# A graph layer on one core: denominator weights 32 columns wide, one block of 32 partitions per tile of nodes

## What is computed

```
Q = elu(q) + 1 ;  K = elu(k) + 1
KV = einsum("nshd,nshv->nhdv", K, v)
Z = 1 / (einsum("nlhd,nhd->nlh", Q, K.sum(axis=1)) + 1e-6)
msg = einsum("nlhd,nhdv,nlh->nlhv", Q, KV, Z)
```

## Time and profile before

| | us |
|---|---|
| median of 3 runs | 1503.72 (1503.57 to 1506.25) |
| the profiled execution, its own time | 1505.46 |
| its span, first to last instruction | 1503.7 |
| PE busy | 1414.6 (94%) |
| PEld busy | 1279.9 (85%) |
| DVE busy | 1151.3 (77%) |
| POOL busy | 953.5 (63%) |
| ACT busy | 759.2 (50%) |
| mean granted TensorE clock | 0.986 |

### The profile page before, as it was taken

One profiled execution on the slowest core, in us unless ns is written; L12 is line 12 of the kernel. 1 busy time (PEld: TensorE's weight loads), 2 busy tenths in 40 slices (PEclk: granted clock), 3 DMA queues, 4 the chain that ended last, 5 costly groups with the idle time before them and its releaser, 6 DMA issues.

```text
span 1503.7 us, 26952 instructions
## 1 busy us (share of the span) xinstructions
PE 1414.6 (94%) x9032; PEld 1279.9 (85%) x9032; DVE 1151.3 (77%) x2565; ACT 759.2 (50%) x1339; POOL 953.5 (63%) x873
## 2 busy tenths in 40 slices
PE   5999999679999999999999999999999999999986
PEld 5999999568888888888888888888888888888875
DVE  6777778558878878787788877788777887878873
ACT  4555555235554445644556445554455445554453
POOL 5777775566775666656676567755677556675452
PEclk9999999899999999999999999999999999999998
DMA  5787765121220212202122112211122111220000
GB/s 175 254 266 230 226 217 194 53 60 49 70 70 23 64 52 69 65 24 62 56 69 62 28 48 69 69 41 48 48 69 69 31 55 52 69 67 24 14 14 14
DMA packets 71630, 121.81 MB, mean 81 GB/s; under 512 B 38053, under 2 KB 42786, under 8 KB 71598
## 3 DMA queue, kind: packets, MB, share of 16 engines
q1 hardware_dynamic: 55598, 108.00, 22.7%
q0 software_dynamic: 16000, 13.43, 4.1%
HBM read 69.47 MB, written 51.70 MB: 81 GB/s over the span
## 4 chain that ended last, share of the span: by engine, by line
PE 62%; DVE 21%; ACT 6%; issue 5%; DVEq 4%; POOL 1%; POOLq 1%; DMA 0%; SPq 0%; ACTq 0%
PE psum L222 18%; PE psum L224 18%; PE psum L223 18%; DVE top_e L1108 6%; PE psum L419 4%; DVE qf L1007 2%; DVE qf L1203 2%; ACT qf L775 2%; DVEq L1056 2%; DVE psum L1128 1%; PE psum L662 1%; ACT relu L789 1%; ACT relu L873 1%; ACT s_hi L790 1%; DVE bn_y L902 1%
## 5 line engine op out<-in xcount | busy, mean ns | idle before, releaser
L1349 POOL TENSOR_TENSOR s_lo<-relu,s_hi 128x1000 fp32r<-128x1000 f32 (+1 forms) x50 | 89.9, 1797 | 150.5 <-ACT s_hi L790 150.5
L222 PE MATMUL psum<-w_hi,h_hi 128*125 128x256 f32 x600 | 172.5, 287 | 5.1 <-DVE h_lo L1229 3.7
L224 PE MATMUL psum<-w_hi,h_lo 128*125 128x256 f32 x600 | 170.1, 283 | 0.0
L223 PE MATMUL psum<-w_lo,h_hi 128*125 128x256 f32 x600 | 169.6, 283 | 0.0
L1343 POOL DMA_INDIRECT xg<-table_xt,idx x100 | 124.7, 1247 | 55.1 <-issue 55.1
L863 ACT ACTIVATE z_hi<-qf 128x500 fp32r<-128x500 f32 x50 | 30.2, 622 | 232.2 <-DVE qf L1203 224.3
L1349 POOL TENSOR_TENSOR h_lo<-relu,h_hi 128x1000 fp32r<-128x1000 f32 x50 | 127.4, 2567 | 29.8 <-ACT h_hi L790 29.8
L1146 DVE SCALAR_TENSOR_TENSOR base<-xb,rn,b_bc 125x256 f32<-125x256 f32 x100 | 144.6, 1486 | 0.3
L1345 POOL DMA_INDIRECT ag<-table_al,idx x100 | 121.3, 1213 | 30.5 <-issue 30.5
L222 PE MATMUL psum<-z_hi,w_hi 128*128 128x500 f32 x300 | 119.8, 399 | 2.3 <-DVE z_lo L1177 2.3
L222 PE MATMUL psum<-xT_hi,w_hi 128*128 128x500 f32 x300 | 120.5, 402 | 1.3 <-ACT h_hi L790 1.3
(11 more groups left out here) (231 smaller groups left out, 4754.1 us busy)
## 6 DMA issues: line engine op xcount, KB each, us to landing
xb<-in_x SPq DMA_DIRECT2D x50, 448.0 KB
xT_hi_table<-x1T_hi SPq DMA_DIRECT2D x25, 500.0 KB
xT_lo_table<-x1T_lo SPq DMA_DIRECT2D x25, 500.0 KB
xT_hi<-xT_hi_table SPq DMA_DIRECT2D x25, 500.0 KB
xT_lo<-xT_lo_table SPq DMA_DIRECT2D x25, 500.0 KB
table_xt<-xts SPq DMA_DIRECT2D x25, 455.0 KB
out<-xmid SPq DMA_DIRECT2D x25, 448.0 KB
xb<-in_x SPq DMA_DIRECT2D x50, 52.0 KB
```

Source lines behind the costliest of these rows:

```text
L222: pe.matmul(out, wh, xh, start=first, stop=False)
L223: pe.matmul(out, wh, xl, start=False, stop=False)
L224: return pe.matmul(out, wl, xh, start=False, stop=last)
L1349: ptt(out, src, hi, ALU.subtract).then_inc(S[done], 1)
```

## The change

Each of the four tiles gets 32 partitions of PSUM of its own. `kden` shrinks to 32 columns per chunk, the 8 head columns written four times, and is the same weight for all tiles. The matmul of tile j writes partitions 32j to 32j+31; the two chunks of a tile add up there, and the loops are swapped (chunks outside, tiles inside). Of each 32 partitions the first 8 serve the rounded value, the next 8 the rest, and the others are not selected by `den_sel`. Which partitions hold a rest is told by a new column `low_rows`, -1 there and 0 elsewhere, so that one instruction over all 128 partitions replaces the subtraction over 64: rdenT = rden_hi * low_rows + rden. The column is made once, ahead of phase 2, by two sums and a multiplication.

```
-KD_STEP = P + 16
+QUAD = 32
...
-        kden = sb("kden", [P, CK, T * KD_STEP])
+        kden = sb("kden", [P, CK, QUAD])
+        low_rows = sb("low_rows", [P, T + 1])
...
+        rden_hi = sb("rden_hi", [P, R + 1], F32R)
...
-                for j in range(T):
-                    for q in range(CK):
-                        last = pe.matmul(psum[:, 6, 0:R], kden[:, q, j * P:(j + 1) * P], tile(qf, q, j),
-                                         start=j == 0 and q == 0, stop=j == T - 1 and q == CK - 1)
+                for q in range(CK):
+                    for j in range(T):
+                        last = pe.matmul(psum[j * QUAD:(j + 1) * QUAD, 6, 0:R], kden[:, q, :], tile(qf, q, j),
+                                         start=q == 0, stop=q == CK - 1)
...
             for q in range(CK):
-                for d in (0, 64):
-                    at = kden[:, q, :].rearrange("p (j n) -> p j n", j=T)[:, :, d + q * per:d + (q + 1) * per]
-                    ts(at, head_mask[:, 0:P:MIX_CH].unsqueeze(1).broadcast_to([P, T, per]), kx[:, q, C:C + 1], None,
-                       ALU.mult)
+                at = kden[:, q, :].rearrange("p (d n) -> p d n", n=MIX_HEADS)[:, :, q * per:(q + 1) * per]
+                ts(at, head_mask[:, 0:P:MIX_CH].unsqueeze(1).broadcast_to([P, QUAD // MIX_HEADS, per]),
+                   kx[:, q, C:C + 1], None, ALU.mult)
...
-                    rows = [d + 16 * j + q * per for d in (0, 64)]
+                    rows = [QUAD * j + d + q * per for d in (0, MIX_HEADS)]
...
+            dve.reduce_sum(low_rows[:, 0:T], ident[:].rearrange("p (j r) -> p j r", r=QUAD)[:, :, MIX_HEADS:2 * MIX_HEADS],
+                           AXX)
+            dve.drain()
+            dve.reduce_sum(low_rows[:, T:T + 1], low_rows[:, 0:T], AXX)
+            dve.drain()
+            ts(low_rows[:, T:T + 1], low_rows[:, T:T + 1], -1.0, None, ALU.mult)
...
-                dve.tensor_copy(rdenT[:, 0:R], rden)
-                dve.drain()
-                tt(rdenT[64:P, 0:R], psum[64:P, 6, P:P + R], rdenT[64:P, 0:R], ALU.subtract).then_inc(S["den_rows"], 1)
+                dve.tensor_copy(rden_hi[:, 0:R], rden)
+                dve.drain()
+                stt(rdenT[:, 0:R], rden_hi[:, 0:R], low_rows[:, T:T + 1], rden, ALU.mult,
+                    ALU.add).then_inc(S["den_rows"], 1)
```

## The result

| | before | changed kernel |
|---|---|---|
| median of 4 runs, us | 1503.67 (1503.57 to 1506.25) | 1511.84 (1510.76 to 1513.25) |
| ratio of the times | | 1.0051, interval 1.0033 to 1.0068 |
| the profiled execution, us | 1505.46 | 1510.76 |
| its span, us | 1503.7 | 1509.0 |
| mean granted clock in it | 0.986 | 0.978 |

The changed kernel is slower by 0.5%, where 1% faster was forecast; the time lies outside the range. Line 1126 of the changed kernel is another instruction, a COPY in `top_weights` that was 1119.

A forecast was written before the change was run, and what follows sets the result against it. Bound by a chain through POOL's e_lo, DVE's line 1108 and ACT that ends PE's 1.5 us hole. -15.4 us (22 x 0.70) + 0.3 us = -15.1 us, from 1503.72 to 1488.6 us; range 1481 to 1504.6.

The forecast's parts named there:

- What bounds the kernel: Each step is set by POOL's e_lo, DVE's line 1108 in top_weights (4.08 us, mostly standing), ACT, then PE.
- the hole: PE's recurring 1.5 us wait before the gb matmuls of line 662, for ACT's gate rows; forecast to shrink to 1.1 us.
- The matmuls: Denominator's 16 records on PE: overlapping tiles gain 0.81 us, a drain takes 0.2, so the denominator is done 0.6 us earlier.
- If 1108 is ahead of `e_lo` it takes 0.17 us: DVE in top_weights: line 1108 passes before POOL's subtractions, line 1114 stands instead till 692.97; 0.75 us gained.
- the -15.4 us: Whole gain in the steps: 22 standing instances of line 1108 times 0.70 us.
- the 0.70 us per step: Gain taken at DVE's line 1108, between branches of 0.75 and 0.62 us, passing on whole to PE's restart.
- The other branch of the forecast: Line 1108 comes up to some 0.35 us into the first e_lo and is let in between the two; 0.62 us gained.
- The new three-operand instruction: On DVE after the denominator, replaces a subtraction of 0.29 us; +0.03 us, not held up beside e_lo.
- Once: Three small DVE instructions ahead of g_lo cost 0.6 us, stage b's first full step gains about 0.3; together +0.3 us.
- Rival 3: At PE's hole: if it outgrows 1.5 us, the clock falls, 22 x 1.6 = 35 us, 1539 us; chance 0.05.
- Rival 1: Denominator matmuls do not overlap, 1108 still ends with e_lo, PE's loss goes into the hole; 1504.3 us; chance 0.26.

The follow-up runs named there:

- e8: Changed kernel with GpSimd's two e_lo subtractions waiting for gate_rows, until the weights of the experts are out; 1439.45 us, ratio 0.9566.
- e9: Kernel before the change with GpSimd's two e_lo subtractions waiting for gate_rows; 1464.25 us, ratio 0.973.
- e5: Changed kernel with the two matmul loops back in the old order, tiles outside and chunks inside; 1511.37 us, one run.
- e6: Changed kernel with all 8 narrow matmuls sent to partitions 0 to 31, leaving out the denominators of three tiles; 1504.0 us, one run.
- e3: Changed kernel with the 8 narrow matmuls issued three times; 1501.99 us, ratio 0.9978.
- e4: Kernel before the change with only the new three-operand instruction and its column low_rows, weights still 128 wide; 1501.17 us, ratio 0.9973.
- e7: Changed kernel with only line 1115, the first instruction of top_weights, moved ahead of one_over_den; 1483.62 us, ratio 0.9862.
- e2: Changed kernel with all of top_weights called ahead of one_over_den on DVE; 1588.12 us, ratio 1.0554.
- e1: Kernel before the change with all of top_weights called ahead of one_over_den on DVE; 1559.89 us, ratio 1.0377.

## Why the prediction was wrong

- **What bounds the kernel: right.** The chain over line 1108 and the hole were read rightly; e8 and e9 show that the hole goes when that line is free. But the prediction called what fills PE ahead of the hole unimportant "as long as the hole is there". It is not unimportant to the clock.
- **The matmuls: mis-sized.** The forecast let two tiles overlap and took 8 x 0.107 us from first to last record. Four overlap: each tile has four records of its own, 0.11 to 0.13 us apart, and the last of 16 starts 0.36 us after the first. The denominator's next reader, line 1133, starts at 0.97 us, not 1.4. The order of the loops, on which the step leaned, gives 0.02 us (e5). The cost of the changes of mode was taken as 0.2 and 0.3 us; it is 0.09 (the matmul before now starts 0.32 us ahead, not 0.23) and 0.17 us (0.20 from the last record to the next matmul, not 0.03; e6 has the same 0.20). So PE saves 1.05 us per step, not 0.3. The Trainium skill ("TensorEngine Tiling (Array Packing)", Key Properties) says that tiles run independently and that a change of mode drains the engine; the trace agrees with both, at those prices.
- **The step that failed: "If 1108 is ahead of `e_lo` it takes 0.17 us", and the -15.4 us built on it.** It came ahead in every step, by 0.15 to 0.29 us, and took 4.82 to 4.95. Its own arrival was not late. So the 0.70 us per step were not gained, and the hole grew to 2.4 us where 1.1 were forecast. What counts is whether the GpSimd instruction is ready in its queue: e8 shows it, with only that changed. The kernel before has the opposite case in each full step: line 1146, also with two inputs in SBUF, starts at 672.07, 0.07 us ahead of an `h_lo` that had itself waited 0.76 us for ACT (672.14 in the earlier trace rows), and passes in 0.47 us, where the two after it take 2.6 us each. That a ready instruction has the port before its recorded start is the reading that fits; the traces do not show the port itself. The other branch of the forecast fails too: the cases of the earlier trace rows, let in between two subtractions, were no model, since in e3 the line comes 0.25 to 0.36 us into the first `e_lo` and stands for both, 4.3 to 4.4 us. Why line 1146 is let in and this line is not was not tried. By the Trainium skill ("SBUF — State Buffer", "SBUF: two separate sides") the pair is a lock, given for the whole instruction to whichever starts first; that is how the forecast was made, and here the measurement decides: the starts in the profile do not tell who has it.
- **The new three-operand instruction: right.** It takes 0.35 us where 0.32 was forecast, and does not stand beside `e_lo` (e4, and line 1142 in e7). That the steps are 0.15 us shorter with it was not foreseen.
- **Once: right.** 0.6 us were expected for the three small instructions ahead of `g_lo`, and they take 0.56 (273.64 to 274.20). `g_lo` starts 1.24 us later than before, but 0.68 us of it were there when the first `den_sel` began (272.02 for 271.34); over all the kernels here that moment lies between 270.98 and 272.16 us, and in e7, with the same three instructions, at 271.09.
- **Rival 3 was the case, at a chance of 0.05.** Its place and its hole (2.3 us forecast, 2.41 measured) are right. It was held back by "in the forecast the hole shrinks", which hung on the failed step. Its price was wrong: the clock fell in 7 of 22 steps at 1.36 us each, not in 22 at 1.6. Why in these 7 was not tried.
- **Rival 1** was right that 1108 ends with `e_lo`, and wrong on why: the records do overlap, and the line is not late. It had PE's loss going into the hole; it was PE's gain, 1.05 us, that did.

## What to carry to other kernels

Time saved ahead of a wait on another engine is not neutral: it makes the wait longer, and where PE's idle time in one piece grew from 1.5 to 2.4 us here, its clock fell in a third of the steps, so shorten what ends the hole first, then PE. When a short DVE instruction stands for a GpSimd one, moving it a little earlier is no cure while the GpSimd instruction is ready in its queue; let GpSimd wait for it, if GpSimd has time to spare (1512 to 1439 us here), and the order of the two queues no longer depends on tenths of a microsecond. Reordering DVE's instructions is only safe if each one that then meets the subtraction has been looked at, COPY and CAST included.

## What the runs showed of the hardware

- **Four matmuls on four groups of 32 columns run at once in plain float32.** 16 records of 125 columns span 0.36 us from first to last start; on one group 1.64 us. With both changes of mode the next matmul comes after 0.56 us and not 1.70. The Trainium skill ("TensorE: Matmul & The Clock Gate", on packing small matmuls) has 2.38 times for three; here four give 3.0.
- **Which DVE instructions stand beside a GpSimd subtraction that is ready in its queue.** One with two SBUF inputs (line 1115; line 1124 in e7), an SBUF to SBUF float32 COPY (line 1126) and a CAST from SBUF to SBUF (line 1123, e2): till the end of both subtractions (line 1146 in the kernel before: of one). A reduction (0.17 us) and a reciprocal (0.18) in e7, and an instruction with one input in PSUM and one in SBUF (0.35): not at all. The start can lie 0.84 us ahead (COPY, e1) or 0.93 us ahead (CAST, e2) and the instruction still stands for 5.5 and 5.6 us.
- **The longer the hole, the more low clock.** With holes of up to 1.7 us in every step it was never seen in the 22 steps. With 2.4 us it came in 7 or 8 of them, for 3.4 us; with 2.8 to 2.9 us (e1) in 15, of which 3 for 6.8 us; with 3.9 to 4.1 us (e2) in all, for 6.8 us in all but the first, beginning 2.0 to 2.5 us into the hole.
